# Cutting the edge sort of a two-layer graph kernel into five parts instead of four

## The chip, the core and the metric

The kernel runs on one core of one Trainium2 chip, as one launch. The metric is the device time of that launch in microseconds. The core has TensorE (PE in the profile, its weight loads PEld), VectorE (DVE), ScalarE (ACT), GpSimd (POOL) and SyncE (SP), which issues most of the DMAs here. POOL issues the indirect DMAs, those that gather or scatter one row per partition by a list of indices.

## What is computed

There are 100000 nodes with 64 features and 50000 edges, sorted by destination, each with a source, 64 features of its own and one of 32 relations. The first layer is a graph convolution, the second an attention over edges that depends on the relation:

```python
h = jnp.maximum(_layernorm(x), 0.0)
x = x + gcn(gcn(h, W1, b1) -> relu, W2, b2)      # both over edge_index, with degrees
h = jnp.maximum(_layernorm(x), 0.0)
h_proj = jnp.einsum('nd,rde->rne', h, relation_weight)
t_r, h_r = h_proj[etype, src], h_proj[etype, dst]
att = jnp.sum(t_r * jnp.tanh(h_r + efeat), axis=-1)
a = softmax of att over the edges of one dst
h_nb = jax.ops.segment_sum(h[src] * a[:, None], dst)
out = leaky_relu((h + h_nb) @ res_w1.T) + leaky_relu(h * h_nb @ res_w2.T)
x = x + out
```

The cost that matters below is `att`. Each edge needs the 64x64 matrix of its own relation, so the kernel first sorts edges by relation: rows with the same relation lie together in tiles of 128, and one matrix serves a tile.

## The kernel before

An edge sits at one of 128 partitions and one of 392 columns (`KE`). Columns are handled 14 at a time (`GT`), which makes 28 steps (`GE`). The stage that the change touches goes through these steps from the last columns to the first. It lies between about 2235 and 3675 us of the profiled execution. What each engine does in step `s` of it:

- **POOL** (`send_rows`, line 1351, and `get_neighbours`, line 1345): scatters the 14 columns of rows of step `s` (edge features, source features, destination features; 192 numbers) into the table `slot_rows`, by 14 indirect DMAs of line 1281; then gathers the source features of step `s + 3` by 14 indirect DMAs of line 1286. I call these scatter `s` and gather `s + 3`. Scatter `s` waits for ACT's copies of scan `s` (line 1548).
- **DVE** (line 944 on): scan `s + 1` (`step_c`: lines 859, 861 and 865, the destination features of a run of edges, filled in backwards); then `sort_next(s)`, a share of the sorting of the next part; then `follow(s)`, a share of scoring and picking.
- **SP** (loop at line 1245): loads the features for scan `s + 1`, then the slot tiles that `follow(s - 1)` scores, then edge features for step `s + 2`. The last load waits until scatter `s` has landed. SP's queue is in order, so the slot tiles of `follow(s)` are issued only after scatter `s` has landed.

The columns are cut into parts at `PART_STEPS`. For each part three things are done on DVE, in this order:

- **Sorting**: 32 counts (`count_edges`, line 639, one for each relation), ten small instructions (`sort_starts`, lines 729 to 740), 32 placings (`place`, lines 750 to 754, and `tile_relation`, line 744: five dependent instructions for each relation), and `slots_found` (8 instructions). They must be done before the part's first scatter. They are spread over the steps of the part before: `steps` in `sort_next` is the number of steps over which the 32 placings are dealt out.
- **Scoring**: a group is four tiles of slots. Its rows are loaded back from `slot_rows` (line 1067), transposed (PE, line 1792), multiplied by the relation's matrix (line 1806), and DVE adds (873), multiplies (882) and sums (883). Three buffers hold loaded tiles (`SB`). A part's first group can be loaded only when all of the part's scatters have landed.
- **Picking**: a pair is two columns of edges. DVE makes one-hot rows (897), PE multiplies them with the scores (1834), and DVE selects (906, twice).

How many groups and pairs stand in which step is computed by `spread_work` from prices (3.0 for a group and 1.9 for a pair) and a room of 35.0 per step; a part may begin one step after its last scatter. What is left is done after the last step (`follow(28)`). A part's number of tiles is its columns plus 31, rounded up to a multiple of 4, since each relation may end in a tile that is not full. `PART_TILES` is 144, 144, 144 and 88 before: 130 groups, and 196 pairs. After the stage, an exponential and the last stage follow, which gathers nothing but writes all results.

Of the kernel before, what the change touches and what calls it, by code (L numbers as in the profile page):

```python
# [46 lines left out]

RG = 4
RW = 3 * D
PART_STEPS = (0, 8, 16, 24, 28)  # L50
PARTS = len(PART_STEPS) - 1
PART_COLS = [(KE - GT * PART_STEPS[k + 1], KE - GT * PART_STEPS[k]) for k in range(PARTS)]
PART_TILES = [-(-(hi - lo + R - 1) // RG) * RG for lo, hi in PART_COLS]
# [13 lines left out]
NBR = 10  # L67
SUM2 = 4
SB = 3
ZW = 1664  # L70
ZN = KS * RW // ZW


# [24 lines left out]
def build(nc, x, src, dst, eattr, etype, w1, b1, w2, b2, relw, rw1, rw2, out):  # L98
    with ExitStack() as ctx:
# [9 lines left out]
        def sems(prefix, names):  # L109
            return {k: sem(f"{prefix}_{k}") for k in names.split()}  # L110
# [72 lines left out]
        def part(buffer, at, shape, dt=F32):  # L183

            n = 1
            for k in shape:
                n *= k
            words = buffer[:, at:at + (n + 1) // 2] if dt == F16 else buffer[:, at:at + n]
            words = words if dt == F32 else words.bitcast(dt)
            if len(shape) == 1:  # L190
                return words
            if len(shape) == 2:
                return words.rearrange("p (a b) -> p a b", b=shape[1])
            return words.rearrange("p (a b c) -> p a b c", b=shape[1], c=shape[2])
# [56 lines left out]
        eti = part(work, W0 + 14 * MM, [KE], I32)  # L251
        mv = part(work, W0 + 14 * MM + 4 * KE + ZW + 3 * KH, [KN, 2])
        zero = part(work, W0 + 14 * MM + 4 * KE, [ZW])

# [92 lines left out]
        pick = sems("pick", "turned lanes spread hot found done")  # L347
# [32 lines left out]
        def step_part(s):  # L380
            return max(k for k in range(PARTS) if PART_STEPS[k] <= s)

# [11 lines left out]
        def spread_work():  # L394


            runs, room = [[] for _ in range(GE + 1)], 0.0
            left = [(k, kind, cost, n) for k in range(PARTS)
                    for kind, cost, n in (("score", 3.0, PART_TILES[k] // RG), ("pick", 1.9, (PART_COLS[k][1] - PART_COLS[k][0]) // 2))]
            at = 0  # L400
            for s in range(GE + 1):
                room = 35.0
                while left and s > PART_STEPS[left[0][0] + 1] or left and s == GE:
                    k, kind, cost, n = left[0]
                    take = min(n - at, max(int(room / cost), 0)) if s < GE else n - at
                    if take == 0:
                        break
                    runs[s].append((kind, k, at, at + take))
                    room, at = room - cost * take, at + take
                    if at == n:  # L410
                        left, at = left[1:], 0
            return runs

        work_at = spread_work()


        @block.vector
        def _(dve):
# [217 lines left out]
            def count_edges(k, r):  # L636
                lo, hi = PART_COLS[k]
                after(dve, counted, k * R + r)
                ts(tmp_b[:, 0:hi - lo], relf[:, lo:hi], rel_no[:, r:r + 1], None, ALU.is_equal, ALU.add,
                   accum_out=cnt[:, 0, r:r + 1]).then_inc(counted, 1)  # L640
# [84 lines left out]
            def sort_starts(k):  # L725
                lo, hi = PART_COLS[k]
                dve.wait_ge(counted, (k + 1) * R)
                dve.wait_ge(prep_pe, 5 + k)
                os.did(ts(pos[:, 0:hi - lo], relf[:, lo:hi], float(R), float(SLOT_SKIP), ALU.is_equal, ALU.mult))
                totals, before = bank(7)[:, 384:384 + R], bank(7)[:, 384 + R:384 + 2 * R]  # L730
                os.do(v.tensor_copy(cnti[:, 0, :], totals))
                os.do(ts(cnti[:, 1, :], cnti[:, 0, :], P - 1, None, ALU.add))
                os.do(ts(cnti[:, 0, :], cnti[:, 1, :], 7, None, ALU.logical_shift_right))
                os.do(v.tensor_copy(cnt[:, 1, :], cnti[:, 0, :]))
                os.do(v.tensor_tensor_scan(out=cnt[:, 2, :], data0=onesk[:, 0:R], data1=cnt[:, 1, :],
                                           initial=0.0, op0=ALU.mult, op1=ALU.add))
                os.do(tt(cnt[:, 3, :], cnt[:, 2, :], cnt[:, 1, :], ALU.subtract))
                os.do(stt(out=cnt[:, 5, :], in0=cnt[:, 3, :], scalar=float(P), in1=before, op0=ALU.mult, op1=ALU.add))
                os.do(ts(cnt[:, 4, :], cnt[:, 5, :], -1.0, None, ALU.add))
                os.do(v.memset(tile_rel[0:1, :], 0.0))  # L740
# [6 lines left out]
            def place(k, r):  # L747
                lo, hi = PART_COLS[k]
                at, one, run = pos[:, 0:hi - lo], tmp_b[:, 0:hi - lo], tmp_b[:, P:P + hi - lo]
                os.do(ts(one, relf[:, lo:hi], rel_no[:, r:r + 1], None, ALU.is_equal))  # L750
                os.do(v.tensor_tensor_scan(out=run, data0=onesk[:, 0:hi - lo], data1=one, initial=cnt[:, 4, r:r + 1],
                                           op0=ALU.mult, op1=ALU.add))
                os.do(tt(run, run, one, ALU.mult))
                os.do(tt(at, at, run, ALU.add))
                if r < R - 1:
                    tile_relation(k, r)

            def slots_found(k):

                lo, hi = PART_COLS[k]  # L760
                at, t0, n = pos[:, 0:hi - lo], PART_TILE0[k], PART_TILES[k]
                pos_i, lanes_i = tmp_b[:, 0:hi - lo].bitcast(I32), tmp_b[:, P:P + hi - lo].bitcast(I32)
                os.do(v.tensor_copy(pos_i, at))
                os.do(ts(lanes_i, pos_i, P - 1, None, ALU.bitwise_and))
                os.do(ts(pos_i, pos_i, 7, None, ALU.logical_shift_right))
                os.do(stt(out=slot_row[:, lo:hi], in0=lanes_i, scalar=float(KS), in1=pos_i, op0=ALU.mult, op1=ALU.add))
                os.did(ts(slot_row[:, lo:hi], slot_row[:, lo:hi], float(t0), None, ALU.add))
                at_step[f"slot rows {k}"] = os.n
                os.did(v.tensor_copy(tile_of[:, lo:hi], pos_i))
                os.did(v.tensor_copy(relf[:, lo:hi], lanes_i))  # L770
                os.did(v.tensor_copy(tile_reli[0:1, t0:t0 + n], tile_rel[0:1, 0:n]))
                os.wait()
                at_step[f"tiles {k}"] = os.n
# [151 lines left out]
            def sort_next(s):  # L925

                k = step_part(s) + 1
                if k == PARTS:
                    return
                first, steps = PART_STEPS[k - 1], PART_STEPS[k] - PART_STEPS[k - 1] - 3  # L930
                n = s - first - 1
                if n == -1:
                    for r in range(R):
                        count_edges(k, r)
                if n == 0:
                    sort_starts(k)
                if 0 <= n < steps:
                    for r in range(n * R // steps, (n + 1) * R // steps):
                        place(k, r)
                if n == steps - 1:  # L940
                    slots_found(k)

            step_c(0)
            for s in range(GE):
                if s + 1 < GE:
                    step_c(s + 1)
                sort_next(s)
                follow(s)
# [115 lines left out]
        def _(sp):  # L1064

            def load(to, of, signal):
                sp.dma_start(to, of).then_inc(signal, 16)
# [115 lines left out]
            def keep_h(g):  # L1183
                sp.wait_ge(G["h"], g + 1)
                load(edge_group(hd_t, g), dh[:, g % 2], d_h[g % 2])
# [10 lines left out]
            for g in range(GE):  # L1196
# [6 lines left out]
                for k in range(g * ZN // GE, (g + 1) * ZN // GE):  # L1203
                    load(lanes[:, k * ZW:(k + 1) * ZW], zero, zeroed)
            keep_h(GE - 1)
# [30 lines left out]
            def load_tiles(s):  # L1236
                for kind, k, lo, hi in work_at[s]:
                    if kind == "score":
                        if lo == 0:
                            for q in range(2):  # L1240
                                sp.wait_ge(c_sent[q], 16 * GT * len(range(q, PART_STEPS[k + 1], 2)))
                        for j in range(lo, hi):
# [684 lines left out]
```

## Time and profile before

| | us |
|---|---|
| three runs | 4298.66, 4302.61, 4294.05 |
| median | 4298.66 |
| the profiled execution, whole | 4327.24 |
| its span | 4325.4 |
| scatter 0 starts | 2292.1 |
| first group of part 0 | 2658.2 |
| scan 27, the last | 3362.4 |
| last pick | 3674.8 |

All times in the text are us from the start of the span of the profiled execution. Its own time is 28.6 us, or 0.7%, above the median of the runs; a difference between two versions is worked out in the profiled execution and then added to the median.

The way to read this profile is by order and not by busy share. Each engine has its instructions in a fixed order. A step takes as long as the engine that is last needs for it: POOL, or the row of work on DVE between one scan and the next. So the interval between two scans, and DVE's idle time inside it, tell which of the two it is.

### The profile page before, as it was taken

The numbers are of one execution on the slowest core, as the hardware profiler recorded it, in microseconds if no ns is written. First come the engines' busy times: TensorE is split into PE (matmuls) and PEld (weight loads), VectorE is DVE, ScalarE is ACT, GpSimd is POOL, SyncE is SP. The second block draws the span as 40 slices with busy tenths as digits, with TensorE's granted clock in tenths as the row PEclk, the third lists the DMA queues.
The fourth block names the chain that finished last, engine by engine and source line by source line (L and its number), as shares of the span: only waits on it lengthen the run. The fifth ranks groups of instructions, "written<-read, shape, count | busy, mean of one in ns | idle before, by whom it ended". The sixth has DMA issues, their size and how long they took to land.

```text
span 4325.4 us, 38668 instructions
## 1 busy us (share of the span) xinstructions
PE 1892.6 (44%) x10654; PEld 1519.8 (35%) x10654; DVE 2696.3 (62%) x5055; ACT 1355.7 (31%) x2808; POOL 2685.7 (62%) x2705
## 2 busy tenths in 40 slices
PE   5700088888856530000000002553553668566663
PEld 2200066666634420000000002452442566565553
DVE  9959967887889865666653423564563454444442
ACT  0012255555533321111110001201301201787773
POOL 8877787400068876777757777557666100487787
PEclk9955578898977765555555555686786796666665
DMA  1137787766534325655642224423523402122220
GB/s 53 37 117 243 238 226 223 214 212 196 189 119 130 113 83 151 212 209 186 215 138 64 74 74 126 141 60 109 147 74 108 122 24 63 47 58 58 58 58 29
DMA packets 353879, 540.59 MB, mean 125 GB/s; under 512 B 207936, under 2 KB 220074, under 8 KB 353670
## 3 DMA queue, kind: packets, MB, share of 16 engines
q1 hardware_dynamic: 271910, 438.60, 31.3%
q0 software_dynamic: 81760, 99.52, 9.6%
q8 instruction: 93, 1.52, 0.1%
q14 instruction: 116, 0.95, 0.1%
HBM read 271.64 MB, written 270.30 MB: 125 GB/s over the span
## 4 chain that ended last, share of the span: by engine, by line
POOL 41%; DVE 17%; issue 15%; PE 13%; DMA 8%; ACT 4%; SPq 1%; POOLq 0%; DVEq 0%; ACTq 0%
POOL arena L1286 20%; POOL result L1281 8%; POOL work L1286 7%; POOL slot_rows L1281 5%; DMA work<-slot_rows 4%; DMA arena<-in_x 3%; PE banks L1834 3%; PE banks L1806 3%; PE banks L1698 2%; DVE spare L906 1%; DVE arena L559 1%; DVE arena L545 1%; PE banks L1792 1%; DVE t_stat L543 1%; DVE t_stat L550 1%
## 5 line engine op out<-in xcount | busy, mean ns | idle before, releaser
L1281 POOL DMA_INDIRECT result<-work,outi x392 | 475.3, 1213 | 455.5 <-DVE work L994 334.2
L1286 POOL DMA_INDIRECT arena<-input_and_place_by_node,src_i x252 | 312.0, 1238 | 471.5 <-DVE arena L677 397.0
L1281 POOL DMA_INDIRECT slot_rows<-work,dsafe x392 | 391.2, 998 | 239.5 <-issue 149.7
L1286 POOL DMA_INDIRECT arena<-g_by_node_and_edge,m_idx x392 | 443.5, 1131 | 121.2 <-issue 119.2
L1286 POOL DMA_INDIRECT work<-in_x,dsafe x392 | 431.5, 1101 | 117.2 <-issue 62.2
L1286 POOL DMA_INDIRECT arena<-h_by_node_and_edge,m_idx x392 | 402.5, 1027 | 119.5 <-issue 119.5
L602 DVE SCALAR_TENSOR_TENSOR work<-work 128x1024 f32<-128x1024 f32 (+1 forms) x77 | 116.7, 1515 | 313.3 <-ACT work L1607 240.7
L1792 PE MATMUL banks<-ident,work 128*128 128x128 f32 x520 | 117.1, 368 | 327.1 <-DMA work<-slot_rows 233.2
L1767 PE MATMUL banks<-last_run,carry 128*128 128x64 f32 x4 | 1.1, 362 | 588.1 <-DVE last_run L825 588.1
L1684 PE MATMUL banks<-ident,arena 128*128 128x128 f32 x392 | 69.2, 305 | 393.5 <-DMA arena<-in_x 392.7
L1698 PEld LDWEIGHTS banks<-w_sb,work 128*128 128x128 f32 x1568 | 206.1, 212 | 84.7 <-issue 84.7
L1895 PE MATMUL banks<-work,ident 128*128 128x65 f32 x784 | 169.5, 411 | 118.8 <-ACT work L1630 118.8
L1698 PE MATMUL banks<-w_sb,work 128*128 128x64 f32 x1568 | 220.0, 300 | 0.0
L906 DVE SCALAR_TENSOR_TENSOR spare<-pos,src_i,banks 128x144 f16<-128x144 f16 (+1 forms) x392 | 139.4, 356 | 119.6 <-PE banks L1834 112.6
L1895 PEld LDWEIGHTS banks<-work,ident 128*128 128x128 f32 x784 | 164.2, 322 | 124.1 <-ACT work L1630 124.1
L859 DVE TENSOR_TENSOR work<-work,ends 128x896 f32<-128x896 f32 x28 | 46.8, 1672 | 258.1 <-DMA work<-h_by_node_and_edge 231.6
L1767 PEld LDWEIGHTS banks<-last_run,carry 128*128 128x128 f32 x4 | 0.8, 252 | 588.2 <-DVE last_run L825 588.2
L1286 POOL DMA_INDIRECT work<-input_and_place_by_node,src_i x140 | 172.4, 1232 | 53.5 <-issue 37.1
L1806 PE MATMUL banks<-work 128*128 x1040 | 198.4, 353 | 13.2 <-ACT work L1553 8.1
L1792 PEld LDWEIGHTS banks<-ident,work 128*128 128x128 f32 x520 | 82.8, 189 | 345.3 <-DMA work<-slot_rows 192.2
L1834 PE MATMUL banks<-spare 128*128 128x144 f32 (+1 forms) x784 | 166.4, 343 | 79.5 <-DVE spare L906 77.6
L1684 PEld LDWEIGHTS banks<-ident,arena 128*128 128x128 f32 x392 | 51.7, 159 | 401.7 <-issue 334.3
(329 smaller groups left out, 6454.1 us busy)
## 6 DMA issues: line engine op xcount, KB each, us to landing
slot_rows<-work SPq DMA_DIRECT2D x60, 832.0 KB, 8.7
work<-slot_rows SPq DMA_DIRECT2D x130, 384.0 KB, 3.5
arena<-in_x SPq DMA_DIRECT2D x96, 512.0 KB, 6.0
input_and_place_by_node<-arena SPq DMA_DIRECT2D x49, 528.0 KB, 2.7
arena<-input_and_place_by_node SPq DMA_DIRECT2D x49, 512.0 KB, 6.6
g_by_node_and_edge<-arena SPq DMA_DIRECT2D x49, 512.0 KB, 2.6
h_by_node_and_edge<-arena SPq DMA_DIRECT2D x49, 512.0 KB
arena<-x_of_destination SPq DMA_DIRECT2D x56, 448.0 KB, 4.2
```

Of the source, the lines that this page charges most:

```text
L543: ot.do(v.tensor_reduce(st[:, 0, :], cols(xin), AX.X, ALU.add))
L602: return stt(out=to, in0=of, scalar=0.01, in1=of, op0=ALU.mult, op1=ALU.max)
L859: oc.did(tt(by_column(pd1)[:, 0:GT, :], cols(phd), wide(ends[:, group(g)], GT), ALU.mult))
L906: stt(out=picked[:, 0:n], in0=tile_no[:, 0:n], scalar=tile_of[:, t:t + 1], in1=bank(7)[:, c * KH:c * KH + n], op0=ALU.is_equal, op1=ALU.mu ...
L1281: pool.indirect_dma_start(out=table[:, :], out_offset=bass.IndirectOffsetOnAxis(ap=idx, axis=0), in_=of, in_offset=None, bounds_check=boun ...
L1286: pool.indirect_dma_start(out=to, out_offset=None, in_=table[:, :], in_offset=bass.IndirectOffsetOnAxis(ap=idx, axis=0)).then_inc(signal, 16)
L1684: ins = transpose(bank(0)[:, k * P:(k + 1) * P], qh0[:, b % 3, half + k * P:half + (k + 1) * P], ident[:])
L1698: ins = matmul(bank(4 + n % 2)[:, k * D:(k + 1) * D], qhid[:, n % 2, at:at + P], w2_sb[:], start=True, stop=True)
L1792: ins = transpose(bank(j % 2)[:, k * P:(k + 1) * P], slot_w[:, j % SB, k, D:RW], ident[:])
L1806: ins = matmul(bank(2 + j % 4)[:, at], slot_ht[:, q, at], flat[:, w], start=True, stop=True)
L1834: ins = matmul(bank(7)[:, c * KH:c * KH + n], lane_hot[:, i % 2, c * P:(c + 1) * P], slot_score[k % 2][:, 0:n], start=True, stop=True)
L1895: ins = matmul(bank(7)[:, 0:DW], ident[:], fmask[:, k, :], start=g == 0 and k == 0, stop=False, skip_group_check=True)
```

## The change

The columns are cut into five parts of 8, 7, 6, 4 and 3 steps instead of four of 8, 8, 8 and 4. `spread_work` gets lower prices and more room, and `sort_next` deals the placings over one more step of the part before (the 2 in place of 3).

```diff
-PART_STEPS = (0, 8, 16, 24, 28)
+PART_STEPS = (0, 8, 15, 21, 25, 28)
...
-ZW = 1664
+ZW = 1668
...
-                    for kind, cost, n in (("score", 3.0, PART_TILES[k] // RG), ("pick", 1.9, (PART_COLS[k][1] - PART_COLS[k][0]) // 2))]
+                    for kind, cost, n in (("score", 2.7, PART_TILES[k] // RG), ("pick", 1.7, (PART_COLS[k][1] - PART_COLS[k][0]) // 2))]
...
-                room = 35.0
+                room = 37.5
...
-                first, steps = PART_STEPS[k - 1], PART_STEPS[k] - PART_STEPS[k - 1] - 3
+                first, steps = PART_STEPS[k - 1], PART_STEPS[k] - PART_STEPS[k - 1] - 2
```

`PART_TILES` becomes 144, 132, 116, 88 and 76: 139 groups. The pairs stay 196. The zeroing of `slot_rows`, in the stage before, takes 64 DMAs instead of 60. What the two tables of numbers give for `follow(s)`, with g for groups and p for pairs, the part ahead of the colon:

| s | before | after |
|---|---|---|
| 9 | 0: 11 g | 0: 13 g |
| 10 | 0: 11 g | 0: 13 g |
| 11 | 0: 11 g | 0: 10 g, 6 p |
| 12 | 0: 3 g, 13 p | 0: 22 p |
| 13 | 0: 18 p | 0: 22 p |
| 14 | 0: 18 p | 0: 6 p |
| 15 | 0: 7 p | none |
| 16 | none | 1: 13 g |
| 17 | 1: 11 g | 1: 13 g |
| 18 | 1: 11 g | 1: 7 g, 10 p |
| 19 | 1: 11 g | 1: 22 p |
| 20 | 1: 3 g, 13 p | 1: 17 p |
| 21 | 1: 18 p | none |
| 22 | 1: 18 p | 2: 13 g |
| 23 | 1: 7 p | 2: 13 g |
| 24 | none | 2: 3 g, 17 p |
| 25 | 2: 11 g | 2: 22 p |
| 26 | 2: 11 g | 2: 3 p; 3: 11 g |
| 27 | 2: 11 g | 3: 11 g, 4 p |
| 28 | 2: 3 g, 56 p; 3: 22 g, 28 p | 3: 24 p; 4: 19 g, 21 p |

The sorting of the new last part (42 columns) stands in `sort_next(21)` (counts), `(22)` (16 placings) and `(23)` (16 placings and `slots_found`), where there was none. That of the part before it (56 columns) moves from steps 16 to 21 to steps 15 to 19, with 8 placings a step instead of 6 or 7.

How the order of instructions moves, first on SP, where the slot tiles of part 1 are first loaded. The rows are the edge features for step 19, the features for scan 18, and the tiles of the first groups. Before:

```order
L1067 DMA work<-in_edge_attr 112x14x64 [waits perm_sent_1]
L1067 DMA work<-in_edge_attr 15x14x64
L1067 DMA work<-in_edge_attr 1x14x64
L1067 DMA work<-h_by_node_and_edge 128x896 [waits perm_run]
L1067 DMA work<-slot_rows 128x768 [waits rel_z,perm_sent_1,perm_sent_0]
L1067 DMA work<-slot_rows 128x768 [waits rel_z] x10
```

After, the same place, where the edge features are those for step 18 and the features those for scan 18 less one:

```order
L1067 DMA work<-in_edge_attr 112x14x64 [waits perm_sent_0]
L1067 DMA work<-in_edge_attr 15x14x64
L1067 DMA work<-in_edge_attr 1x14x64
L1067 DMA work<-h_by_node_and_edge 128x896 [waits perm_run]
L1067 DMA work<-slot_rows 128x768 [waits rel_z,perm_sent_1,perm_sent_0]
L1067 DMA work<-slot_rows 128x768 [waits rel_z] x12
```

The tiles follow scatter 16 instead of scatter 17 (`perm_sent_0` is signalled by even scatters), and 13 of them stand in a row instead of 11.

Second, DVE between the last pairs of part 1 and the first groups of part 2. Before, where scans 25 and 26 follow one another and then scoring starts:

```order
L906 SCALAR_TENSOR_TENSOR spare,relf<-pos,src_i,banks 128x144 x4
L859 TENSOR_TENSOR work<-work,ends 128x14x64
L861 COPY work<-work 128x64
L865 SCALAR_TENSOR_TENSOR work<-work 128x960
L859 TENSOR_TENSOR work<-work,ends 128x14x64
L861 COPY work<-work 128x64
L865 SCALAR_TENSOR_TENSOR work<-work 128x960
L873 TENSOR_TENSOR dsti<-banks,work 128x256
```

After, where a step's scan is followed by placings. These are the rows behind the 13 groups of `follow(22)`: scan 24 and the first of 16 placings, which stand ahead of the groups of `follow(23)`:

```order
L883 TENSOR_REDUCE spare<-tmp_a 128x4
L859 TENSOR_TENSOR work<-work,ends 128x14x64
L861 COPY work<-work 128x64
L865 SCALAR_TENSOR_TENSOR work<-work 128x960
L750 TENSOR_SCALAR tmp_b<-relf,rel_no 128x42
L751 SCALAR_TENSOR_TENSOR tmp_b<-onesk,cnt,tmp_b 128x42
L753 TENSOR_TENSOR tmp_b<-tmp_b 128x42
L754 TENSOR_TENSOR pos<-pos,tmp_b 128x42
L744 SCALAR_TENSOR_TENSOR tmp_b<-pos,cnt,tmp_b 1x76
```

The new part's placings stand in DVE's row between scans that had nothing between them before.

## Rows read from the trace of the kernel before

**Rows 1.** Line 865 (the scan) in 2350:2580, then stretch 2404 to 2442 of all engines.

```profile
L865 DVE TENSOR_TENSOR_SCAN work<-work x6: 2157/2157/2158, 2356.3 to 2543.1; 128x960 f32<-128x960 f32 x6
...
core 0: us, PE busy (x) PEld busy (x) DVE busy (x) ACT busy (x) POOL busy (x), PEclk, DMA share, GB/s
2404.40:2441.80 37.40, 0.00 (x0) 0.00 (x0) 15.82 (x39) 3.49 (x3) 28.86 (x28) 0.50 0.26 73
```

**Rows 2.** Timeline of DVE: line 859, where scans 12, 17, 25 and 27 begin.

```profile
2740.18 1.66 DVE L859 TENSOR_TENSOR work<-work,ends 128x896 f32<-128x896 f32 x1
...
2944.01 1.67 DVE L859 TENSOR_TENSOR work<-work,ends 128x896 f32<-128x896 f32 x1
...
3275.53 1.70 DVE L859 TENSOR_TENSOR work<-work,ends 128x896 f32<-128x896 f32 x1
...
3362.36 1.68 DVE L859 TENSOR_TENSOR work<-work,ends 128x896 f32<-128x896 f32 x1
```

**Rows 3.** Timeline: scatters 12, 16, 17 begin (POOL); part 1's first group (DVE).

```profile
2746.72 1.03 POOL L1281 DMA_INDIRECT slot_rows<-work,dsafe  x1 [10.22 <-ACT work L1548]
...
2933.49 1.02 POOL L1281 DMA_INDIRECT slot_rows<-work,dsafe  x1 [0.30 <-issue]
...
2972.24 1.02 POOL L1281 DMA_INDIRECT slot_rows<-work,dsafe  x1 [0.30 <-issue]
...
3002.55 0.42 DVE L873 TENSOR_TENSOR dsti<-banks,work 128x256 f32<-128x256 f32 x1 [27.67 <-PE banks L1806]
```

**Rows 4.** Stretches in which DVE idles behind part 0.

```profile
2974.95:3002.60 27.65, 4.11 (x18) 3.69 (x19) 0.05 (x1) 1.17 (x2) 21.26 (x22) 0.50 0.42 133
3279.50:3290.30 10.80, 0.00 (x0) 0.00 (x0) 0.04 (x1) 3.48 (x3) 8.36 (x9) 0.50 0.50 128
3294.20:3333.20 39.00, 4.13 (x18) 3.66 (x19) 0.05 (x1) 3.71 (x4) 29.87 (x31) 0.50 0.38 118
3366.30:3371.20 4.90, 2.55 (x12) 2.56 (x13) 0.02 (x1) 2.67 (x3) 1.69 (x2) 0.50 0.06 22
```

**Rows 5.** Stretches of scoring: 11, 11, 3, 25 and 22 groups.

```profile
2658.15:2691.00 32.85, 21.36 (x116) 19.59 (x114) 12.88 (x34) 10.15 (x22) 24.93 (x27) 0.78 0.59 163
2706.25:2740.20 33.95, 21.82 (x108) 19.09 (x107) 13.01 (x34) 10.19 (x21) 23.16 (x24) 0.74 0.56 152
...
2804.40:2810.35 5.95, 2.29 (x9) 1.88 (x9) 3.61 (x9) 2.61 (x6) 4.54 (x5) 0.63 0.24 82
...
3371.20:3446.45 75.25, 49.15 (x283) 43.66 (x282) 29.37 (x75) 22.98 (x49) 12.10 (x13) 0.81 0.49 144
3546.70:3610.45 63.75, 42.07 (x248) 35.80 (x246) 25.79 (x66) 20.44 (x43) 0.00 (x0) 0.87 0.41 118
```

**Rows 6.** Stretches of picking: 18, 56 and 28 pairs.

```profile
2854.30:2888.30 34.00, 25.20 (x144) 21.93 (x144) 20.92 (x91) 0.00 (x0) 18.16 (x19) 0.86 0.19 46
...
3447.20:3545.05 97.85, 69.26 (x452) 59.90 (x452) 64.18 (x280) 0.39 (x1) 0.00 (x0) 0.97 0.01 2
3611.20:3674.80 63.60, 61.49 (x220) 50.90 (x220) 31.07 (x140) 0.00 (x0) 0.00 (x0) 0.50 0.08 30
```

**Rows 7.** Stretches of sorting: 32 counts, starts, 6 placings (112 columns), 6 (56), `slots_found`.

```profile
2947.85:2957.80 9.95, 0.00 (x0) 0.00 (x0) 8.84 (x65) 3.48 (x3) 7.67 (x8) 0.50 0.42 99
2963.60:2965.85 2.25, 0.00 (x0) 0.00 (x0) 1.91 (x11) 2.21 (x2) 1.72 (x2) 0.50 0.09 15
2694.80:2706.25 11.45, 5.78 (x26) 5.34 (x27) 10.43 (x31) 3.73 (x4) 8.79 (x9) 0.50 0.54 185
...
3039.20:3048.30 9.10, 4.34 (x19) 3.89 (x20) 8.05 (x32) 3.72 (x4) 6.97 (x8) 0.50 0.63 215
...
2852.50:2854.30 1.80, 0.00 (x0) 0.00 (x0) 1.65 (x8) 0.00 (x0) 1.19 (x3) 0.50 0.16 55
```

**Rows 8.** The page's DMA issues: the zeroing; and a stretch of the stage before.

```profile
slot_rows<-work SPq DMA_DIRECT2D x60, 832.0 KB, 8.7
...
2100.00:2200.00 100.00, 0.00 (x0) 0.00 (x0) 67.26 (x88) 17.48 (x20) 78.97 (x70) 0.50 0.57 199
```

## Prediction

> **What bounds the kernel now.** The change touches one stage, and three things decide how long it takes. I read the pace of the scans first, then what fills DVE's row between two scans, then where DVE idles.
>
> From scan 3 to scan 8 a step takes 37.4 us: POOL's 14 scatters and 14 gathers fill it, and DVE is busy for under half of it [rows 1]. There POOL is last, and DVE work put between two scans costs nothing until DVE's row is as long as 37.4 us. Where groups and pairs stand, the row is longer: between scan 12 and scatter 12 lie 6.5 us, and POOL had idled 10.2 us for it [rows 2, 3]. There DVE is last, every instruction in its row counts in full, and POOL's 37.4 us of that step are cover that DVE gets at no cost. So the stage up to scan 27 is a sum over steps of the longer of the two, and behind scan 27 [rows 2] POOL has almost nothing left, and DVE's row of 47 groups and 84 pairs runs alone to 3674.8 [rows 6].
>
> The last piece is how each part's scoring starts. It needs the part's scatters, and SP issues the tiles behind the wait for the newest scatter. From the start of scatter 17 to the first group of part 1 lie 30.3 us [rows 3], in which DVE idles 27.65 us; ahead of part 2 it idles 10.8 and 39.0 us, ahead of the tail 4.9 us. Together 82.4 us behind part 0 [rows 4].
>
> **Prices.** Scan, three instructions: 3.9 us (3275.53 to the idling at 3279.50) [rows 2, 4]. Groups: 11 take 32.85 and 33.95 us, 3 take 5.95, so beyond the first three, which have been loaded ahead, one costs (33.4 - 5.95) / 8 = 3.43 [rows 5]. A run of 13 is 40.3, of 10 is 30.0, of 7 is 19.7. In the tail a group costs 75.25 / 25 = 3.01, later 63.75 / 22 = 2.90 [rows 5]. Pairs: 1.89 among scans, 1.75 in the tail at a granted clock of 0.97, 2.27 at 0.50 [rows 6]; among scans I take 1.87. Placings: 1.91 with 112 columns, 1.52 with 56, so by a straight line 1.71 with 84 and 1.42 with 42; 32 counts with 56 columns take 9.95, so about 9.5 with 42, the starts 2.25, `slots_found` 1.8 [rows 7].
>
> **Part 0, its row of work.** Its first group stays at 2658.15 [rows 5], since steps 0 to 9 keep their order and POOL's pace. Before, 285.9 us later scan 17 begins [rows 2]. After, the same 36 groups and 56 pairs stand in fewer steps: groups 40.3 + 40.3 + 30.0 = 110.6 instead of 3 x 33.4 + 5.95 = 106.2 (+4.4, a shorter run gets more of its tiles ahead); one scan less (-3.9); 26 placings with 84 instead of 112 columns (-5.2). Scan 16 begins at 2658.15 + 281.2 = 2939.3. That is the point: nearly the same time, but one step behind, and that step's 37.4 us of POOL must still be paid.
>
> **Part 1.** It needs scatter 16 only. Scan 15 lies 6 pairs and a scan ahead of scan 16, at 2924.2; scatter 15 at 2930.7 (+6.5), scatter 16 38.7 later as before [rows 3], 2969.4; first group 30.3 later, 2999.7 instead of 3002.55. Its row took 273.0 us up to scan 25 [rows 2]. After: 33 groups (-5.9), 7 pairs fewer (-13.1), scans 18 to 21 instead of 19 to 24 (-7.8), 24 placings instead of 26 (-3.0): 243.2 us. Scan 22 begins at 3242.9. DVE is 33 us earlier than before, and three scans behind.
>
> **Parts 2 to 4 up to scan 27.** Before, scans 25 and 26 and then 11 groups, with 50 us idle. Now scan 22 and the new part's counts: 3.9 + 9.5, to 3256.3. Scan 23, starts, 16 placings of 1.42: 3.9 + 2.25 + 22.7, to 3285.2. Scatter 22 can start at 3249.4, its tiles would allow a group at 3279.7, so the placings are last by 5 us and the idling is gone. Then:
> - 13 groups, 40.3: scan 24 at 3325.5
> - 3.9 + 22.7 + 1.8 + 40.3 = 68.7: scan 25 at 3394.2
> - 3.9 + 5.95 + 17 pairs 31.8 = 41.7: scan 26 at 3435.9
> - 3.9 + 22 pairs 41.1 = 45.0: scan 27 at 3480.9
>
> Before, it was at 3362.4 [rows 2]: 118.5 us late.
>
> **The tail.** Before, 312.4 us from scan 27 to the last pick. After: scan 3.9, 3 pairs 5.6, 22 groups of part 3 66.2 (3.01), 28 pairs 49.0 (1.75), 19 groups of part 4 55.1 (2.90), 21 pairs 47.7 (2.27, as the last ones before), idling 1 (4.9 before; 0 to 4.9), small gaps 3.1 (what the rows of before leave over): 231.6 us. The tail is shorter by 80.8 us; that is what the fifth part gives. Part 4's groups would come 124.7 us after scan 27 begins, and scatter 27 allows them after 6.5 + 30.3, so its wait is covered.
>
> **Zeroing.** Four more DMAs of 8.7 us each, in a stage where POOL issues 70 gathers in 100 us and the DMA engines are busy to 0.57 [rows 8]. The last step of that stage has three of them either way. I take 0; the cover is POOL's own row. The other end is 4 x 8.7 = 35 us, if each put its landing on the path; nothing waits for one of them alone, so I stay near 0 and allow 5.
>
> **Sum.** 118.5 - 80.8 = 37.7 us later. The last stage takes the same instructions, so this stands to the end: 4327.2 + 38 in a profiled execution, and 4298.7 + 38 = 4336.4 for the median. Unlike the sum, its cause is simple: DVE gets 9 groups (27 us) and the fifth part's sorting (59 us), less 5 for narrower placings, and 82 us of idle time is all there is to hide 81 us of new work. The new numbers use 60 of them and turn steps that POOL had paid for into steps that DVE pays for.
>
> **Two rules of the Trainium skill.** The placings hardly get cheaper with fewer columns: half the columns leave 80% of the price [rows 7]. "VectorE: DVE Perf Modes", section on the TRN2 errata, says that an operation from SBUF pays a fixed cost and then one cycle or less an element; the trace agrees. An estimate by that page's formula has four instructions of a placing save 73 ns each from 112 to 42 columns, 1.62 us instead of 1.42, which would make the sum 6 us larger. It speaks against cutting into more parts.
>
> The last 28 pairs kept PE busy for 61.5 of 63.6 us and had half the clock throughout [rows 6]. "TensorE: Matmul & The Clock Gate", part 1, says that activity releases the throttle. By it the last 21 pairs would run at the full clock, 1.75 us each, and the sum would be 27 us, 4326; the row disagrees, and the sum goes by the row. Inside the forecast's 84% I give that case 25, since the clock did stand at 0.97 for the 56 pairs before.
>
> **Rivals.**
> - Faster: the idle time is used up and the tail's gain is kept. Its best case hides 81 us of work in 82 us of idling (-1) and has the last pairs at the full clock (28 x 0.52 = -15): 4283. It decides the matter if scan 27 comes less than 81 us late, before 3443. For it: pairs among scans ran at up to 0.9 of the clock. Against it: the wait behind scatter 16 remains, and steps 23 to 26 show no idling left to fill. 3%.
> - No difference: the placings of step 23 and the run shapes cost nothing, because PE and not DVE sets the pace of groups and the placings fit beneath loads: 24.5 + 5.5 us less, 4307. Against it: 6 placings and then 11 groups took their full sum, 11.45 + 33.95 [rows 5, 7]. 4%.
> - Slower still: all pairs of the tail at 2.27 (+15) and the zeroing at its 5 us, or group runs of 13 that meet POOL's DMAs: 4356 to 4365. 8%.
> - The change does not do what it says: a part's slots are found after POOL wants its first scatter, and POOL waits. Part 4's would be found at 3325.5 + 3.9 + 22.7 + 1.8 = 3353.9, scatter 25 comes at 3400.7, 47 us later. Not a wait, unless I misplace a step; then up to 37 us more, 4373. 1%.
>
> **How the numbers follow.** Forecast 84%, 4336. Downward: the last pairs at 1.75 (-11), groups beyond the eleventh at 3.01 (-4), idling 0 (-1), the runs' own spread (about -4): 4316. Upward: the tail's other pairs at 2.27 (+15), zeroing (+5): 4356. That range leaves out the two cases that are not slower and most of the two that are slower still, some 15%. A measurement of this kernel tells about 0.2%, 8.6 us, from no change. Faster 3%, within 4%, slower 93%.
>
> **What would show it.** Scan 16 at about 2939 and scan 22 at about 3243: else my run prices are wrong. Scan 24 to scan 25 at 69 us, scan 27 near 3481. No idling of DVE over 5 us between scans 22 and 27. From scan 27 to the last pick 232 us, with the last 21 pairs in 37 or 48 us by the clock. If scan 27 comes before 3443, the cover that I count as lost was not, and the kernel is faster.

## The result, and the profile after

The changed kernel takes 4390.11 us (median of 4374.51 to 4396.02), the kernel before 4299.86 (4294.05 to 4302.61): a ratio of 1.0196, interval 1.0175 to 1.0217. It is 90 us slower, where 38 were forecast; the range ended at 4356. The pair was measured again beside other kernels (e18 below): 4390.9 against 4311.5, 1.0198 (1.0168 to 1.0229). The ratios with an interval are those on record; they differ by up to 0.002 from the quotient of the two medians, and a difference in us below is one of medians.

The page of the changed kernel, its span and two of the costliest groups. POOL's scatters wait 248 us for ACT's copies of the scans, and a product with the scores (line 1834) takes 386 ns on average, where it took 343 before:

```profile
span 4394.2 us, 39306 instructions
...
L1281 POOL DMA_INDIRECT slot_rows<-work,dsafe x392 | 392.1, 1000 | 368.2 <-ACT work L1548 248.1
...
L1834 PE MATMUL banks<-spare 128*128 128x144 f32 (+4 forms) x784 | 191.5, 386 | 50.2 <-DVE spare L906 47.6
```

Who waited in the stage, for the kernel before (stretch 2300 to 3400) and then for the changed one (2300 to 3520). The columns are us in total, times, and the longest:

```profile
POOL slot_rows L1281 <- issue: 147.9, 378, 30.6
POOL slot_rows L1281 <- ACT work L1548: 89.8, 8, 16.9
```

```profile
POOL slot_rows L1281 <- ACT work L1548: 248.1, 12, 36.1
```

The one wait of 30.6 us that the kernel before has under "issue" stands ahead of scatter 27, and the view of line 1548 (who waited for it) counts it among the waits for ACT's copies:

```profile
  POOL slot_rows L1281: 120.4, 9
```

So POOL waits for DVE's row in twelve steps instead of nine, and 128 us longer. The timeline of DVE in the changed kernel, where scans 16, 22, 24, 25, 26 and 27 begin, answers [rows 2]:

```profile
2934.26 1.67 DVE L859 TENSOR_TENSOR work<-work,ends 128x896 f32<-128x896 f32 x1
...
3234.86 1.67 DVE L859 TENSOR_TENSOR work<-work,ends 128x896 f32<-128x896 f32 x1
...
3317.30 1.66 DVE L859 TENSOR_TENSOR work<-work,ends 128x896 f32<-128x896 f32 x1
...
3382.68 1.66 DVE L859 TENSOR_TENSOR work<-work,ends 128x896 f32<-128x896 f32 x1
...
3437.27 1.67 DVE L859 TENSOR_TENSOR work<-work,ends 128x896 f32<-128x896 f32 x1
...
3488.02 1.67 DVE L859 TENSOR_TENSOR work<-work,ends 128x896 f32<-128x896 f32 x1
```

Scan 27 is 125.7 us late against [rows 2], about what POOL waits longer. The rest is in stretches of the changed kernel (the columns are those of [rows 1]). In order: 13 groups, 17 pairs and 22 pairs of part 2, 22 groups and 28 pairs of part 3, 19 groups and 21 pairs of part 4:

```profile
2658.80:2695.20 36.40, 22.81 (x140) 18.31 (x138) 15.26 (x40) 12.57 (x25) 27.85 (x29) 0.92 0.64 173
...
3400.80:3437.20 36.40, 34.51 (x136) 30.29 (x136) 19.73 (x84) 0.00 (x0) 5.34 (x6) 0.51 0.11 30
3441.10:3488.00 46.90, 44.87 (x176) 39.27 (x176) 25.60 (x110) 3.39 (x3) 13.77 (x14) 0.50 0.19 65
...
3502.40:3569.60 67.20, 43.76 (x249) 39.17 (x247) 25.87 (x66) 20.01 (x43) 7.74 (x8) 0.81 0.49 138
3570.40:3634.50 64.10, 61.31 (x225) 50.99 (x226) 31.09 (x140) 0.00 (x0) 0.00 (x0) 0.51 0.00 2
3637.40:3694.10 56.70, 38.25 (x213) 33.09 (x211) 22.42 (x57) 17.33 (x37) 0.00 (x0) 0.82 0.41 112
3694.90:3742.40 47.50, 45.46 (x165) 37.98 (x164) 22.79 (x105) 0.00 (x0) 0.00 (x0) 0.50 0.11 39
```

Read the column with the granted clock, the third from the end. In [rows 6] only the last 28 pairs of the kernel before had 0.50, at 2.27 us each. Here every pair of parts 2, 3 and 4 has it (the lower of the two levels, 1.2 GHz of 2.4), 91 of 196. They cost 2.1 to 2.3 us, but for three pairs between a scan and groups that cost 2.5, and TensorE is busy for 95% of the stretches and more. With 47.5 us the last 21 pairs are at the half clock too. The pairs of part 1 are only a little narrower, 98 partitions and 132 columns, and they get the full clock once a run of them has gone on for a while. 22 pairs and then 17:

```profile
3159.30:3201.20 41.90, 33.73 (x176) 29.31 (x176) 25.43 (x111) 0.00 (x0) 18.63 (x20) 0.76 0.16 37
3204.90:3234.90 30.00, 21.15 (x132) 18.23 (x132) 19.28 (x87) 3.39 (x3) 20.49 (x21) 0.90 0.33 84
```

### The profile page after: what moved, and what is told of

Read it like the earlier page. It is cut to its first block, busy times and chain, and to the rows that moved or that the text cites. A ratio compares the mean times of both kernels' runs of the same rounds, so it can differ in the third digit from the quotient of the medians.

```text
span 4394.2 us, 39306 instructions
## 1 busy us (share of the span) xinstructions
PE 1967.3 (45%) x10767; PEld 1582.0 (36%) x10767; DVE 2749.2 (63%) x5323; ACT 1364.4 (31%) x2827; POOL 2677.3 (61%) x2705
## 4 chain that ended last, share of the span: by engine, by line
POOL 39%; DVE 16%; PE 16%; issue 14%; DMA 9%; ACT 4%; SPq 1%; POOLq 0%; DVEq 0%; ACTq 0%
POOL arena L1286 20%; POOL result L1281 8%; POOL work L1286 7%; DMA work<-slot_rows 5%; POOL slot_rows L1281 4%; PE banks L1834 4%; DMA arena<-in_x 4%; PE banks L1806 3%; PE banks L1825 3%; PE banks L1698 2%; PE banks L1792 1%; DVE arena L559 1%; DVE arena L545 1%; DVE t_stat L543 1%; DVE t_stat L550 1%
## 5 line engine op out<-in xcount | busy, mean ns | idle before, releaser
L1825 PE MATMUL banks<-pos,ident 112*128 112x128 f32 (+4 forms) x784 | 181.7, 373 | 84.2 <-DVE spare L897 72.2
L1834 PE MATMUL banks<-spare 128*128 128x144 f32 (+4 forms) x784 | 191.5, 386 | 50.2 <-DVE spare L906 47.6
L906 DVE SCALAR_TENSOR_TENSOR spare<-pos,src_i,banks 128x144 f16<-128x144 f16 (+4 forms) x392 | 132.9, 339 | 128.8 <-PE banks L1834 121.7
```

What stands on the lines that cost most here:

```text
L906: stt(out=picked[:, 0:n], in0=tile_no[:, 0:n], scalar=tile_of[:, t:t + 1], in1=bank(7)[:, c * KH:c * KH + n], op0=ALU.is_equal, op1=ALU.mu ...
L1825: ins = matmul(bank(6)[:, c * P:(c + 1) * P], ident[0:n, at:at + 1].to_broadcast([n, P]), lanes_t[0:n, :], start=True, stop=True)
L1834: ins = matmul(bank(7)[:, c * KH:c * KH + n], lane_hot[:, i % 2, c * P:(c + 1) * P], slot_score[k % 2][:, 0:n], start=True, stop=True)
```

## The experiments

Two theories stood after the result. **Clock**: picking in parts with fewer columns and fewer tiles makes smaller products (84, 56 and 42 instead of 112 partitions in one, 116, 88 and 76 instead of 144 columns in the other), and in a row of such pairs TensorE is not granted the full clock. **Numbers**: the fuller steps end a part earlier and leave POOL's time uncovered. The rival to both was that the fifth part's own work costs all of it.

### The spread of executions: e1

The kernel before, unchanged.

> The kernel before, unchanged, profiled once more beside its own timed runs. Open point: its first profiled execution took 4327 us where its timed runs took 4294 to 4303, and the changed kernel's profile (4396) lies within its timed runs. Theory 'clock': the same program has executions that differ in which stretches TensorE gets its full clock; a profile near 4300 should show the last 28 pairs at about 1.75 us (49 us, not 63.6) or other stretches at the full clock, and scan 27 near 3362. Rival 'chip': the whole execution is a little slower everywhere, for instance POOL's gathers; then every stage differs by the same 0.7% and scan 27 lies near 3340.

Measured: 4308.0 us against 4311.7 for its twin's runs, which reach from 4290 to 4322. The profiled execution took 4314. Its last 28 pairs had 2.27 us at 0.50 again, scan 0 came 6 us earlier than in the first profile, scan 27 10 us earlier (3352.6) and the last pick 14. So the time is not lost in one place, and the clock of the last pairs is not what differs; a profile near 4300, which the theory 'clock' spoke of, was not taken. All runs of this kernel at this speed lie between 4290 and 4328. The three runs from which the forecast started are on the low side of that; 11 of the 90 us are that.

### Picks at full size: e2 and e3

e2 gives the product with the scores all 144 columns:

```diff
-        slot_score = [part(spare, 0, [PART_TILES[0]]), part(spare, PART_TILES[0], [PART_TILES[1]])]
-        S0 = PART_TILES[0] + PART_TILES[1]
+        slot_score = [part(spare, k * KH, [KH]) for k in range(2)]
+        S0 = 2 * KH
...
-                    ins = matmul(bank(7)[:, c * KH:c * KH + n], lane_hot[:, i % 2, c * P:(c + 1) * P], slot_score[k % 2][:, 0:n],
+                    ins = matmul(bank(7)[:, c * KH:c * KH + KH], lane_hot[:, i % 2, c * P:(c + 1) * P], slot_score[k % 2][:, 0:KH],
```

> The changed kernel, but every product of picking takes 144 columns of scores on TensorE, also in parts 1 to 4, where only 132, 116, 88 and 76 of them are used; DVE still reads only those. It adds work to TensorE and takes none away. Theory 'narrow picks lose the clock': the 91 pairs of parts 2 to 4 ran at 2.08 to 2.23 us with the clock at 0.5, where the 105 of parts 0 and 1 mostly had 1.63 to 1.69; with full width they return to about 1.7, the last pick comes 30 to 45 us earlier, the kernel takes 4345 to 4365. Rival 'the clock follows something else' (how long TensorE has worked before, or the stage): the pairs stay at the half clock and get wider products, 2.2 to 2.3 us each, the kernel takes 4390 to 4405.

e3 has that, and 112 partitions in the product that spreads the lanes (`PW` is 112; the transpose and the copy ahead of it are as wide, and the transpose waits for the last pair of the part before):

```diff
-                n = PART_COLS[k][1] - PART_COLS[k][0]
+                n = PW
                 after(pe, pick["hot"], i)
```

> As e2_after_wide_scores, and the other product of picking, which spreads one column's lanes over the partitions, contracts over 112 partitions in every part instead of 112, 98, 84, 56 and 42; the rows beyond a part's own meet zeros of the identity. Theory 'narrow picks lose the clock': as in e2 or better, if the number of partitions in use counts too; 4340 to 4360. Rival 'something else': 4390 to 4405, since the time of that product does not depend on its partitions.

Measured: e2 4390.0 us, 1.0189 (1.0137 to 1.0240) of the kernel before; e3 4354.3 us, 1.0096 (1.0059 to 1.0134). So e3 gives 36 us back against e2 and the change, with more work on TensorE, and e2 nothing. Stretches of e2, in order 16 pairs and 21 pairs of part 2, 27 of part 3, 20 of part 4:

```profile
3396.00:3424.00 28.00, 20.75 (x132) 17.84 (x130) 17.82 (x83) 0.00 (x0) 3.98 (x5) 0.94 0.13 35
3430.00:3473.00 43.00, 37.87 (x171) 33.21 (x170) 24.11 (x108) 1.53 (x2) 13.82 (x14) 0.66 0.19 69
3555.00:3622.00 67.00, 64.72 (x217) 51.26 (x217) 29.64 (x135) 0.00 (x0) 0.00 (x0) 0.50 0.00 1
3685.00:3733.90 48.90, 47.55 (x159) 37.36 (x157) 21.70 (x102) 0.00 (x0) 0.00 (x0) 0.50 0.06 25
```

The same pairs in e3:

```profile
3412.00:3440.00 28.00, 20.82 (x132) 17.88 (x130) 17.89 (x83) 0.00 (x0) 4.15 (x5) 0.94 0.13 35
3446.00:3482.00 36.00, 26.62 (x171) 22.94 (x170) 23.10 (x107) 1.52 (x2) 13.81 (x14) 0.95 0.23 81
3561.00:3610.50 49.50, 39.82 (x225) 34.69 (x226) 28.73 (x137) 0.00 (x0) 0.00 (x0) 0.83 0.00 1
3674.00:3708.30 34.30, 26.91 (x163) 23.23 (x162) 20.93 (x104) 0.00 (x0) 0.00 (x0) 0.90 0.14 52
```

With 144 columns alone, part 2 (84 partitions in the other product) gets the full clock for a part of the time, and parts 3 and 4 (56 and 42) not at all; there the wider product at the half clock makes pairs dearer, about 2.5 us instead of 2.3. With 112 partitions as well, all of them get it, and a pair costs 1.7 to 1.8 us. So the columns alone changed the clock in part 2, and the partitions did in parts 3 and 4. Partitions at full size beside narrow scores were not run, so whether they alone would do is open. The clock theory holds for e3. The time of e2 is its rival's number, but not for the rival's reason: e2 gained in part 2 and lost it again in parts 3 and 4.

### The numbers: e4, and three kernels beside one another: e18, e19, e20

e4 is the changed kernel with the old prices and room; e19 is the same kernel again.

```diff
-                    for kind, cost, n in (("score", 2.7, PART_TILES[k] // RG), ("pick", 1.7, (PART_COLS[k][1] - PART_COLS[k][0]) // 2))]
+                    for kind, cost, n in (("score", 3.0, PART_TILES[k] // RG), ("pick", 1.9, (PART_COLS[k][1] - PART_COLS[k][0]) // 2))]
...
-                room = 37.5
+                room = 35.0
```

> Five parts of 8, 7, 6, 4 and 3 steps as in the changed kernel, but the old prices (3.0, 1.9) and room (35.0): groups and pairs spread over more steps, 60 groups... of the tail fewer are moved forward: behind scan 27 stand 11 + 30 groups and 49 pairs instead of 41 groups and 52 pairs. Theory 'parts': the loss comes from the fifth part (its 9 groups, its sorting, its narrow pairs), and the numbers matter little: 4375 to 4395. Rival 'numbers': the loss comes from fuller steps, which end sooner and leave POOL's time uncovered: then 4330 to 4350.

Measured: 4359.6 us, 1.0110 (1.0068 to 1.0153). It lies between the two forecasts: the numbers cost about 30 us, and five parts with narrow picks still cost 48. Then three kernels beside one another: e18 the changed kernel, e19 with the old numbers, e20 with the old numbers and picks at full size. In e20, as in the kernels e6, e7, e9, e12 to e15 and e17 below, the transpose and the copy keep their size, and the partitions beyond a part's own hold older numbers that meet zeros of the identity.

> The changed kernel as it is, beside the two that follow on one chip. On a chip like the first ones 80 to 95 us above the kernel before. On one with the 11% longer times: if the causes are the same, 80 to 110 us above it.

> As e4. Theory 'numbers': 25 to 40 us below e18. Rival 'the parts alone': within 10 us of e18.

> As e9. Theory 'two causes add': 25 to 40 us below e19. Rival 'they overlap': less than 15 us below e19, since with the old numbers fewer narrow pairs would stand where only DVE works.

| kernel | us | to the kernel before (4311.5) |
|---|---|---|
| e18, the change | 4390.9 | 1.0198 (1.0168 to 1.0229) |
| e19, old numbers | 4359.8 | 1.0122 (1.0096 to 1.0149) |
| e20, old numbers, full-size picks | 4308.0 | 1.0001 (0.9982 to 1.0021) |

The change costs 79 us here, just short of the 80 to 95 expected. The numbers cost 31 us, the narrow picks 52, together 83, and what is left of the change is within 0.2% of the kernel before. 52 is more than the 25 to 40 expected and than the 36 of e3. In the profiled executions the pairs of parts 2 to 4 took 202, 161, 200 and 158 us (the change, e3, e19, e20), so full-size picks made them cheaper by 42 us with either set of numbers. Six more lie in the last 19 groups, 54.4 us at a granted clock of 0.97 in e20 against 60.1 at 0.82 in e19; the rest is open.

The kernel before is no clean measure for e20, though, since its own last 28 pairs are narrow too, 63.6 us [rows 6]. At full size the same 28 took 46.6 us (e6 below, whose tail runs at the usual pace: its 56 pairs of part 2 took 96.7 us, against 97.85 in [rows 6]). An estimate from these: with full-size picks four parts would take some 17 us less than 4311.5, so the fifth part's own work costs about 14 us in e20, and only 35 of the 52 us are what the change itself added in narrow picks. Then 31, 35 and 14 make up the 79, but for rounding. Four parts with full-size picks were not run beside e20.

The pairs of parts 3 and 4, in the tails of e19 and e20 (27 or 28 of part 3, then 20 or 21 of part 4), first e19:

```profile
3536.00:3598.00 62.00, 61.14 (x224) 50.93 (x225) 30.52 (x138) 0.00 (x0) 0.00 (x0) 0.51 0.00 1
3659.00:3704.70 45.70, 44.26 (x164) 36.88 (x163) 22.28 (x104) 0.00 (x0) 0.00 (x0) 0.51 0.10 39
```

then e20:

```profile
3511.00:3556.00 45.00, 34.24 (x224) 29.43 (x222) 28.42 (x139) 0.83 (x2) 0.00 (x0) 0.96 0.00 1
3612.00:3645.30 33.30, 25.53 (x159) 21.90 (x157) 20.39 (x104) 0.00 (x0) 0.00 (x0) 0.93 0.10 41
```

In e20 these pairs cost 1.6 to 1.7 us each at 0.90 to 0.96; in e3 part 3's had 0.83 and cost 1.8, since the clock rose only after the first third of them. Why it rose later there is open.

Where the numbers' 31 us lie is seen at the start of part 1. In the changed kernel DVE has finished part 0 one step early and then idles until POOL has scattered part 1's last rows:

```profile
2969.60:2994.40 24.80, 4.06 (x18) 3.64 (x19) 0.00 (x0) 1.17 (x2) 18.86 (x20) 0.50 0.46 137
```

In e20, with the old numbers, scans 17 and 18 are 49.8 us apart with 11 groups between them, and the groups follow the placings without a wait; e19 is alike:

```profile
2929.90:2979.70 49.80, 23.68 (x132) 19.83 (x132) 29.48 (x89) 14.10 (x25) 38.22 (x39) 0.76 0.56 155
```

With fewer groups and pairs in a step, part 0's row still fills the step in which POOL scatters part 1's last rows. Filled steps do not save the work that they take from that step: they turn it into idle time, 24.8 us here, with a further 3.3 at scan 17. What e19 gains beyond that up to scan 27 is work that it has moved behind it, 14 pairs, and its tail is longer by about as much.

### Runs in which every kernel took 11% longer

Four parts with the change's numbers (e5, e11, e16), the kernel before with full-size picks (e6, e12), the kernel of e20 (e9, e13, e15), that of e6 with a room of 25 (e7, e14), and parts of 5, 7, 8 and 8 steps with a room of 25 and full-size picks (e17) ran beside kernels before that took 4796, 4821 and 4799 us. The record does not show what set these runs apart: chip number 7 stands beside 4312 us and beside 4799. In them DVE and ACT stop again and again for what the profile does not show. The timeline of e12 within part 0's groups, DVE:

```profile
2912.25 0.42 DVE L874 TENSOR_TENSOR dinv_e<-banks,work 128x256 f32<-128x256 f32 x1 [12.27 <-remote]
...
2927.74 0.42 DVE L874 TENSOR_TENSOR dsti<-banks,work 128x256 f32<-128x256 f32 x1 [14.28 <-remote]
```

A step with 11 groups takes 68 to 72 us there instead of 44 to 49, so what is the longer row in a step is decided otherwise. I read from these runs only ratios to their own kernel before.

```diff
-PART_STEPS = (0, 8, 16, 24, 28)
+PART_STEPS = (0, 5, 12, 20, 28)
...
-ZW = 1664
+ZW = 1572
...
-                room = 35.0
+                room = 25.0
...
-                first, steps = PART_STEPS[k - 1], PART_STEPS[k] - PART_STEPS[k - 1] - 3
+                first, steps = PART_STEPS[k - 1], PART_STEPS[k] - PART_STEPS[k - 1] - 2
```

(the diff of e17 beside its full-size picks; e7 has the room alone, e5 the prices and the 37.5 of the change).

> The kernel before with the change's prices (2.7, 1.7) and room (37.5) alone; four parts and the same 130 groups and 196 pairs, dealt out in fuller steps, so that parts 0 and 1 end one step sooner. Theory 'cover': a step that DVE fills beyond POOL's 37 us is paid by DVE, and the step it leaves empty is paid by POOL, so two emptied steps cost up to 2 x 37 us less what DVE idled there: scan 27 at 3415 to 3435 and the kernel at 4350 to 4380. Rival 'sum': the same instructions take the same time wherever they stand; 4305 to 4320.

> The kernel of e5 once more. In the call of e5, e6, e7 and e9 every kernel, the one before too, took 11% longer (4796 us), with stalls of 8 to 20 us in which several engines waited for nothing that the profile shows, so its steps can't be compared with those of the other calls. Expected as there: theory 'cover' 4350 to 4380 against 4300 to 4312 for the kernel before, scan 27 at 3415 to 3435; rival 'sum' 4305 to 4320.

> Four parts with the change's prices and room. Theory 'cover': two steps that POOL pays for alone come in front, DVE idles more ahead of parts 1 and 2, scan 27 at 3415 to 3435, 40 to 70 us above the kernel before. Rival 'sum': within 10 us of it.

1.0083, 1.0074 and 1.0073 (the last 1.0051 to 1.0094): 31 to 45 us. The numbers do harm without a fifth part too, so the rival 'sum' falls, at this speed; two of the three lie below the 40 to 70 expected.

> The kernel before, with both products of picking at their full size in every part: 144 columns of scores, 112 partitions (rows beyond a part's own hold older numbers that meet zeros). Only part 3's 28 pairs change. Theory 'narrow picks lose the clock': they go from 2.22 us at the clock 0.50 to 1.7 at 0.8 or more, the last pick comes 10 to 15 us earlier; 4293 to 4303. Rival: what was seen in the changed kernel came from the order of stages there; the pairs stay at 2.2 to 2.4 us, 4308 to 4320.

> The kernel of e6 once more, for the same reason. There part 3's 28 pairs went to 1.60 us at the clock 0.97, and the ratio to the kernel before was 0.998. Theory 'narrow picks lose the clock': 10 to 16 us less than before. Rival: within 3 us of it.

0.9981 (0.9959 to 1.0004) and 0.9966 (0.9939 to 0.9992). The last 28 pairs, which had the clock 0.50 and 2.27 us in the kernel before, cost 1.66 us in both. In e6:

```profile
4088.50:4135.10 46.60, 34.67 (x220) 29.97 (x220) 29.02 (x140) 0.00 (x0) 0.00 (x0) 0.94 0.11 39
```

> Five parts, old prices and room (as e4_five_parts_old_numbers), both products of picking at full size. With e6 it leaves the fifth part's own work: 9 groups, its sorting, less the narrower placings. Theory 'two causes add': the clock costs 36 us with either set of numbers and the numbers 30, so this one takes 4318 to 4335 and lies 20 to 35 us above e6. Rival 'they overlap', since pairs among scans lie partly beside POOL's time: 4340 to 4350.

> The kernel of e9 once more, for the same reason. Theory 'two causes add': 20 to 35 us above e12; the fifth part's own work costs that. Rival 'they overlap': 40 to 60 us above e12.

> Five parts, old prices and room, both products of picking at full size. Theory 'two causes add': 10 to 25 us above the kernel before; the fifth part's own work, 9 groups and 59 us of sorting, mostly not hidden. Rival 'they overlap': 35 to 50 us above it, as e4.

1.0103, 1.0119 and 1.0101, 49 to 54 us above the kernel before, where the same kernel is level with it at the other speed (e20). Against four parts that have full-size picks as well, they are 61 us (e9 against e6) and 69 us (e13 against e12) slower. That is the fifth part's own work at this speed, far more than the 14 estimated above. Steps with groups are longer here, so nine more groups may cost more; that was not taken apart.

> The kernel before with a room of 25 instead of 35 (steps with 8 groups or 13 pairs) and both products of picking at full size. Theory 'cover': the opposite of the change's step. Steps that DVE fills to about POOL's 37 us use all of POOL's time; scan 27 comes at 3240 to 3270, though more groups and pairs are left for the tail; last pick 60 to 80 us earlier than before, 4225 to 4255. Rival 'tail': what is left for the tail costs as much as it saves ahead of scan 27: 4290 to 4310.

> The kernel of e7 once more, for the same reason. Theory 'cover': scan 27 at 3240 to 3270, the kernel 60 to 80 us below the kernel before. Rival 'tail': within 20 us of the kernel before.

> Four parts of 5, 7, 8 and 8 steps, old prices, a room of 25, placings dealt out as in the change, both products of picking at full size; 131 groups. Theory 'cover': part 0 ends three steps earlier, so that POOL's time in steps 6 to 9 covers groups too, and no step holds much more than POOL's 37 us: scan 27 at 3260 to 3290, last pick near 3570 to 3600, 60 to 100 us below the kernel before. Rival 'tail': the tail has 36 groups and 80 pairs more work of its own kind and takes back what the front gives; within 20 us of the kernel before.

0.9969 (0.9936 to 1.0002), 0.9985 (0.9954 to 1.0016), and 0.9961 (0.9936 to 0.9986) for e17, 16 us less than before. Gains of 60 us and more were expected. e7 and e14 gain not clearly more than full-size picks alone do (e6, e12): 8 us less than e6, 12 us more than e12. Most of the steps of 8 groups take 57 to 63 us in these runs, far over POOL's 37, so the thing to be tested, steps that fit beneath POOL's time, did not come about. Whether they gain more at the other speed was not measured.

## Why the prediction was wrong

The sign came out as forecast, and so did the mechanism of rows, steps and POOL's paid step. The size did not: 90 us instead of 38, outside the range. The step that failed is the price of the pairs of parts 2 to 4. By the forecast's own steps, in the profiled execution:

- **Part 0 and part 1, right.** Scan 16 at 2934.3 (2939.3 forecast), scan 22 at 3234.9 (3242.9). A step behind at nearly the same time, as worked out. Runs of 13 groups cost 36.4 to 39.9 us and not 40.3: beyond the third group 3.43 us each was too much for the ones added. The idling ahead of part 1, in which the 31 us of the numbers mostly lie, is in the forecast's sum as the step of POOL that must still be paid.
- **Placings of the new part, right.** Scan 24 at 3317.3 and scan 25 at 3382.7, 65.4 us apart instead of 68.7; 16 placings took 22.8 to 23.3 us (22.7). DVE's idling ahead of part 2 is gone.
- **Scan 25 to 26, wrong by 12.9 us.** 54.6 instead of 41.7. 8.4 of them are a wait I had in [rows 4] as the 4.9 us ahead of the tail and did not place here. SP loads the tiles behind the wait for the scan, and in every step that I priced from, placings stood between scan and groups and hid it; this step has none. e20 has 8.9 us at the same place, and no wait over 5.3 in the groups of the two steps before, which have placings. The timeline of DVE in the changed kernel:

```profile
3395.03 0.42 DVE L873 TENSOR_TENSOR dinv_e<-banks,work 128x256 f32<-128x256 f32 x1 [8.44 <-PE banks L1806]
```

- **Pairs of parts 2 to 4, wrong by 27 us.** This is the term that failed. I took 1.87 us among scans and 1.75 for the 28 pairs of part 3 in the tail, from rows of pairs with 112 partitions and 144 columns [rows 6]; at the half clock they cost 2.14 (17 pairs), 2.13 (22), 2.5 (3) and 2.29 (28). That is 4.6 + 5.8 + 1.8 + 15.1 us. The upper bound in the text had the 15 for the tail and nothing for the pairs among scans. The row of 28 pairs at 2.27 was there; I set it aside as a matter of when the clock stands low, where a difference in kind, 56 partitions and 88 columns, stood in the program. Full-size picks gave these pairs the full clock back (e3, e20). That the last 21 pairs came out at 47.5 us against 47.7 forecast is because their price was taken from that row of narrow ones.
- **The tail** was 254.4 us and not 231.6, 17 of it the pairs; the rest is two gaps of 3 us ahead of groups, and groups at 3.05 and 2.98. **Scan 27** at 3488.0 and not 3480.9 is the two errors above less the cheaper groups.
- **From profile to median.** The last pick is 67.6 us late in the profile (37.7 forecast) and the span 68.8. The other 21 us of the 90 are the spread of executions, which the range took as about 4: the profiled one of the kernel before lay high, the three runs low. In the second measurement of the pair (e18) the difference is 79. So the miss of 52 us is 30 in the sum, nearly all of it the pairs, and 21 here. With the difference of e18 the miss would still be 41 us, and outside the range.
- **The two rules.** Small operations do have a fixed cost: 16 placings with 42 columns took 1.43 to 1.46 us each, near the 1.42 taken from rows, and the estimate of 1.62 was too high. The rule from the Trainium skill, "TensorE: Matmul & The Clock Gate", part 1, that activity releases the throttle, had the last 21 pairs at the full clock; they had 0.50 with TensorE busy for 96% of the stretch, so that case fell. In e20 the same pairs had 0.93 with TensorE busy for 77%. So here the busy time that the profile shows did not tell which clock a stretch would get, and a reader can't take it for the activity that the rule speaks of.
- **Rivals.** None took place. 'Slower still' had the right sign and named the half clock, but ended at 4365 with 8%; the pairs among scans and the 8.4 us wait were missing in it.

That the numbers and the narrow picks account for most of the loss is shown by e19 and e20: without them the five parts are level with the kernel before. It does not show that the fifth part is free, since the kernel before pays for 28 narrow pairs of its own; by the estimate above about 14 us remain for its groups and sorting.

## What to carry to other kernels

When a price is taken from a row, take it from a row with the same shape, or price the shape. Cutting work into smaller parts makes smaller products, and in this case TensorE stayed at its half clock over them, though it was busy; padding the products to their full size was faster. When a variant with a repair is compared with the old kernel, ask whether the repair would help the old one too. Filling a step of a pipeline beyond the other engine's time only pays if the step that it empties is needed for nothing: look at what the emptied step waits for.

## What the runs showed of the hardware

- Runs of 17 pairs and more whose two products had 112 partitions and 144 columns got a granted clock of 0.83 to 0.97 and took 1.6 to 1.9 us a pair ([rows 6], e3, e20, and the last pairs of e6, at 0.94); with 98 and 132 it was 0.76 and 0.90 and 1.8 to 1.9 us. At 84 and 116, 56 and 88, 42 and 76 they had 0.50 and 2.1 to 2.3 us, with TensorE busy for 95% and more. In the changed kernel more work on TensorE (e3) made the stretches of parts 2 to 4 shorter by a fifth, and e20 did the same against e19.
- With 144 columns but 84 partitions (e2) two runs had 0.94 and 0.66, with 56 and 42 partitions 0.50 and about 2.5 us a pair.
- One program took 4312 us in some runs and 4796 to 4821 in others, with waits of DVE of 12 and 14 us that the profile puts down to nothing on the core; the order of two kernels changed with it (e20's kernel: level with the kernel before, and 1% slower). What decides between the two is not known.
